# Keys and values of the fourth layer projected side by side, with a key's scaling behind the row maximum

## The chip, the cores and the metric

The kernel runs on one core of one Trainium2 chip. The metric is device time in microseconds. Five engines share the work: PE (TensorE) multiplies matrices into PSUM, DVE (VectorE) and ACT (ScalarE) read PSUM and work elementwise, POOL (GpSimd) works on SBUF alone, SP (SyncE) issues the DMAs. Each runs its own queue in order, and semaphores tie the queues together.

## What is computed

Two sequences of 256 tokens of 512 channels pass four layers, each `x + tanh(g) * attention(layernorm(x), context)` and then `x + tanh(g') * ffn(layernorm(x))`. The context has 512 rows per sequence. The change touches the attention of the fourth layer alone (32 query heads, 8 key/value heads, head size 128):

```
q = rmsnorm(hidden @ Wq.T, q_norm_w);  k = rmsnorm(context @ Wk.T, k_norm_w);  v = context @ Wv.T
rmsnorm(x, w) = x * rsqrt(mean(x*x over the 128 channels of the head) + 1e-5) * w
out = softmax(q k' / sqrt(128) + mask) v @ Wo.T
```

## The kernel before, in words

**Precision.** Every float32 matrix product is three products in fp32r: an operand is split into hi (rounded by ACT in a copy) and lo (the rest, a subtraction on DVE or POOL). The helper `three` (L365 to L372) issues hi x hi, lo x hi, hi x lo for each 128 rows of contraction. So all those matmuls have line L370.

**Tiling.** A group is one key/value head with its four query heads h = 0 to 3. The layer has 8 groups. A head has four slots j = 0 to 3, one for each 128 query rows (two per sequence). In a slot (h, j) PE does, in this order: the scores of the slot two ahead (3 matmuls of 512 columns, psS), the four transposes of this slot's probabilities (psT), at j = 0 and j = 2 the weighted sum of values for half a head (12 matmuls of 256 columns, psO), at one slot a head the projection of queries (12 of 512, psQ), and then the units of `plan(h, j)`, which use the two psX banks in turn.

**Units.** `prep` in the table ATTN names the units that make the next group's keys and values. "k" and "v" project into a tile with one channel per partition and 512 context rows across (12 matmuls of 512 columns). For the keys, ACT squares (L1131), DVE multiplies by k_norm_w into scr (L972); unit "m" sums the squares over the channels by 4 small matmuls with a tile of ones (L816), DVE and POOL turn the sums into 1/rms (L974, L1230), POOL builds diagonal tiles of it (L1234), unit "b" spreads them over the partitions by a float32 matmul (L820, two passes), DVE multiplies (L976), ACT and DVE split into hi and lo (L1138, L943). For the values, DVE copies (L982), unit "t" transposes (L811), and ACT and DVE split (L1150, L985). Units "q" (L825) are the same sums of squares for the queries; units "out" project a finished group to the output.

**What sets the order.** All of it is written out: `head` of each engine walks the same slots, and `walk` puts the groups in a hardware loop of two groups per turn (three turns) between a first and a last part; the loop goes back between slots (1,3) and (2,0). A use of a psX bank waits for the use two before it to be freed (`x_free`). The first group's units run in the prologue, one behind the other with nothing beside them. In a slot DVE does: row maximum of the slot two ahead (mask addition L897, maximum L901), the low part of the transposed probabilities (L913), the reciprocal of the row sum (L909), o_low at j = 0 (L937), then units. ACT does: high part of the transposes (L1099), exponential (L1092), o_high (L1121), units, high parts of weights. POOL does: the normalizing of a row (L1213), units, low parts of weights (1.3 us each).

Of the kernel before, what the change touches and what calls it, by code (L numbers as in the profile page):

```python
# [21 lines left out]
F32 = mybir.dt.float32  # L22
# [52 lines left out]
         prep={(1, 3): ["k0"], (2, 0): ["k1", "m0"], (2, 1): ["m1"], (2, 2): ["b0"], (2, 3): ["v0", "b1"],  # L75
               (3, 0): ["t0"], (3, 1): ["v1"], (3, 2): ["t1"]}),
# [9 lines left out]
            "av_mm o_hi o_lo x_mm x_act x_free k_f k_hi k_lo k_r k_diag").split()  # L86
# [44 lines left out]
class Layer:  # L131


    def __init__(self, index, sems):
# [24 lines left out]
        act_uses = len([u for u in self.flat if u[0] in ("t" if self.masked else "kt")])  # L159
# [6 lines left out]
                     k_f=self.n_k * n if self.masked else 0, k_hi=self.n_k * n if self.masked else 0,  # L166
                     k_lo=self.n_k * n if self.masked else 0, q_f=4 * n if self.masked else 0,
                     q_sum=4 * n if self.rope else 0, q_r=4 * n if self.rms else 0,
                     k_r=2 * n if self.rms else 0, k_diag=2 * n if self.rms else 0)
# [5 lines left out]
         self.x_free, self.k_f, self.k_hi, self.k_lo, self.k_r, self.k_diag) = counters  # L175
# [91 lines left out]
def program(nc, a, out, scratch):  # L267

    ctx = ExitStack()
    with ctx:  # L270
# [102 lines left out]


# [341 lines left out]
        def attn_tensor(pe, L):  # L716
# [160 lines left out]
        def attn_vector(dve, L):  # L877
# [67 lines left out]
            def use(g, what, gp):  # L945
# [6 lines left out]
                act_letters = "t" if L.masked else "kt"  # L952
                if kind == "t" or (kind == "k" and not L.masked):
                    L.x_act.wait(dve, L.count(g, act_letters, what))
                elif kind == "k" and L.rms:
                    L.k_f.wait(dve, L.count(g, "k", what))
# [68 lines left out]
            def head(g, h):  # L1025
                for j in range(L.slots):
                    nxt = L.step(g, h, j, L.ahead)
                    if nxt:
# [23 lines left out]
                    while late and late[0] in before:  # L1052
                        k_low(*late.pop(0))
# [25 lines left out]
        def attn_scalar(act, L):  # L1079
# [43 lines left out]
            def use(g, what, gp):  # L1123
# [3 lines left out]
                if kind in "kb":  # L1127
                    k_hi = k_cols(gp.par, i * CTX, CTX)[0]
                if kind == "k" and L.rms:
                    L.x_mm.wait(act, k + 1)  # L1130
                    L.k_f.inc(act.activation(ksq[:, i, :], X, ACT.Square))  # L1131
                elif (kind == "k" and L.rope) or kind == "b":

                    if L.rope:
                        L.k_f.wait(act, L.count(g, "k", what))
                    else:
                        L.x_free.wait(act, k + 1)
# [29 lines left out]
            def head(g, h):  # L1167
                for j in range(L.slots):
# [14 lines left out]
                    for u in L.slot_uses(g, h, j):  # L1183
                        if u[0] == "b" or (u[0] == "k" and L.rope):
# [673 lines left out]
```

How the kernel before makes its waits and increments, by code:

```python
    def wait(self, eng, value):  # L121
        if isinstance(value, int) and value <= 0:
            return
        eng.wait_ge(self.sem, value + self.base)
# [233 lines left out]
        def after(dve, ins):  # L359
            own[0] += 1
            ins.then_inc(dve_self, 1)
            dve.wait_ge(dve_self, own[0])
# [27 lines left out]
        def start_vector(dve):  # L391
            for c in range(1, DC):
                dve.wait_ge(ctx_hi, c + 1)
                dve.tensor_tensor(cT_lo[:, c, :], ctx_f[c], cT_hi[:, c, :].bitcast(F32),
                                  ALU.subtract).then_inc(ctx_lo, 1)
# [1 line left out]
        def start_scalar(act):  # L397
            act.wait_ge(gate_dma, 32)
            act.activation(gates[:, :], gates[:, :], ACT.Tanh).then_inc(gate_done, 1)
# [1 line left out]
        def start_ctx_high(act, c):  # L401
            act.wait_ge(ctx_dma[c], 16)
            act.activation(cT_hi[:, c, :], ctx_f[c], ACT.Copy).then_inc(ctx_hi, 1)
# [1 line left out]
        def start_gpsimd(pool):  # L405
            pool.wait_ge(ctx_hi, 1)
            pool.tensor_tensor(cT_lo[:, 0, :], ctx_f[0], cT_hi[:, 0, :].bitcast(F32), ALU.subtract).then_inc(ctx_lo0, 1)
# [8 lines left out]
        def dq_sync(sp, g, h):  # L416
            if g is not None and (h or g.off or g.loop is not None):
                sp.wait_ge(dq_done, g.at(4, h))
                sp.dma_start(scratch[:, bass.ds(g.address(4 * DQ, (h - 1) * DQ), DQ)], dq_w).then_inc(dq_out, 16)
            if g is None:
                sp.dma_start(dq_codes[0], a["codes"][:, 0:DQ]).then_inc(dq_code[0], 16)
# [997 lines left out]
        def f1_tensor(pe):  # L1420
            pe.wait_ge(ln_lo, 4 * NT)
```

## Time and profile before

| what | value |
|---|---|
| median of 3 runs | 2134.17 us (2130.99 to 2135.35) |
| the profiled execution | 2134.03 us, its span 2132.1 us |
| mean granted TensorE clock in the span | 0.966 |
| instructions | 33124 |

The span runs from the first to the last instruction. Busy shares are merged times of an engine. Matmuls overlap in the records, so the distance between starts tells more than a duration. A row of the timeline has the start, the duration, the engine, the line, the operation with its tiles, and in brackets the idle time ahead of it with what ended it. A row of the table by stretch has the stretch, its length, then for PE, PEld (PE's weight loads), DVE, ACT and POOL the busy time with the number of instructions, then the granted clock, the busy share of the DMA engines, and GB/s. The granted clock is 1.0 at 2.4 GHz and 0.5 at 1.2 GHz.

### The profile page before, as it was taken

The page shows a single profiled execution, that of the slowest core. Times are in us where ns is not written, and L with a number is a line of the kernel's source. Part 1 is how long each engine was busy: PE and PEld are TensorE (multiplying, and loading weights), DVE is VectorE, ACT ScalarE, POOL GpSimd, SP SyncE. Part 2 cuts the span into 40 slices and gives each one's busy share as a digit, 9 for nine tenths or more (in the row PEclk, how much of TensorE's full clock was granted, in tenths as well). Part 3 has the DMA queues.
Part 4 walks back from the last instruction along what each step waited for, and adds up shares of the span by engine and source line. Part 5 has one row for each costly group of instructions (what it writes and reads, how often), then busy time and mean ns, then how long its engine had stood idle before and what let it go on. Part 6 is the DMA issues. An engine that isn't in the chain of part 4 may idle for free.

```text
span 2132.1 us, 33124 instructions
## 1 busy us (share of the span) xinstructions
PE 1966.9 (92%) x10874; PEld 1653.4 (78%) x10874; DVE 1428.9 (67%) x2532; ACT 1035.1 (49%) x2268; POOL 951.7 (45%) x975
## 2 busy tenths in 40 slices
PE   5999999999748999998988999998799999999997
PEld 4788888888537888886766888887588888888886
DVE  5777777777768878887234555556466776677676
ACT  3766676666315545543123544542255555455442
POOL 2655555554536656663322332323154444344532
PEclk9999999999869999999988999999899999999999
DMA  3212222221301111111210101001110110111001
GB/s 141 75 46 81 84 74 78 57 74 55 99 35 54 56 54 52 61 48 51 73 48 4 34 15 28 23 1 56 55 32 30 45 46 22 40 45 45 16 20 46
DMA packets 47068, 106.76 MB, mean 50 GB/s; under 512 B 6064, under 2 KB 21936, under 8 KB 43104
## 3 DMA queue, kind: packets, MB, share of 16 engines
q1 hardware_dynamic: 46944, 105.14, 15.7%
q8 instruction: 74, 1.21, 0.2%
q14 instruction: 50, 0.41, 0.1%
HBM read 98.37 MB, written 6.75 MB: 49 GB/s over the span
## 4 chain that ended last, share of the span: by engine, by line
PE 70%; DVE 15%; issue 7%; ACT 6%; POOL 2%; DVEq 0%; ACTq 0%; POOLq 0%
PE psX L370 24%; PE psQ L370 12%; PE psS L370 12%; PE psO L370 11%; PE psT L755 6%; PE psT L370 1%; DVE pT_lo L913 1%; DVE p_sb L897 1%; DVE nbias L901 1%; ACT pT_hi L1099 1%; ACT dq_space L449 1%; ACT p_sb L1088 1%; DVE nbias L891 1%; PE psX L825 1%; ACT p_sb L1092 1%
## 5 line engine op out<-in xcount | busy, mean ns | idle before, releaser
L1213 POOL TENSOR_SCALAR p_sb<-p_sb,rrec 128x512 f32<-128x512 f32 (+1 forms) x320 | 267.0, 834 | 690.2 <-DVE rrec L909 690.2
L1099 ACT ACTIVATE pT_hi<-psT 128x512 fp32r<-128x512 f32 (+2 forms) x384 | 234.9, 612 | 349.6 <-PE psT L755 348.0
L913 DVE TENSOR_TENSOR pT_lo<-psT,pT_hi 128x512 fp32r<-128x512 f32 (+2 forms) x384 | 270.9, 705 | 107.0 <-ACT pT_hi L1099 106.4
L370 PE MATMUL psO<-pT_hi,v_hi 128*128 128x256 f32 (+1 forms) x832 | 254.6, 306 | 24.1 <-DVE pT_lo L913 18.1
L755 PE MATMUL psT<-ident,p_sb 128*128 128x128 f32 x1600 | 244.9, 278 | 14.2 <-POOL p_sb L1213 10.7
L755 PEld LDWEIGHTS psT<-ident,p_sb 128*128 128x128 f32 x1600 | 197.4, 143 | 52.8 <-POOL p_sb L1213 15.8
L370 PE MATMUL psO<-pT_lo,v_hi 128*128 128x256 f32 (+1 forms) x832 | 237.3, 285 | 0.0
L370 PE MATMUL psO<-pT_hi,v_lo 128*128 128x256 f32 (+1 forms) x832 | 237.1, 285 | 0.0
L370 PE MATMUL psQ<-xnT_hi,wq_hi 128*128 128x512 f32 (+1 forms) x448 | 189.3, 422 | 14.8 <-DVE qscr L875 9.2
L370 PE MATMUL psS<-kT_hi,q_hi 128*128 128x512 f32 (+2 forms) x448 | 177.1, 395 | 18.0 <-ACT p_sb L1092 16.1
L1092 ACT ACTIVATE p_sb<-psS,nbias 128x512 f32<-128x512 f32 (+1 forms) x192 | 145.3, 757 | 81.0 <-DVE nbias L903 81.0
L370 PE MATMUL psQ<-xnT_hi,wq_lo 128*128 128x512 f32 (+1 forms) x448 | 180.1, 402 | 0.0
L370 PE MATMUL psQ<-xnT_lo,wq_hi 128*128 128x512 f32 (+1 forms) x448 | 179.9, 402 | 0.0
L370 PEld LDWEIGHTS psO<-pT_hi,v_hi 128*128 128x128 f32 (+1 forms) x832 | 155.2, 187 | 31.1 <-DVE pT_lo L913 27.1
L370 PE MATMUL psX<-wo_hi,oT_hi 128*128 128x512 f32 (+1 forms) x432 | 172.9, 400 | 0.0
L370 PE MATMUL psX<-wo_hi,oT_lo 128*128 128x512 f32 (+1 forms) x432 | 169.5, 392 | 0.0
L370 PE MATMUL psX<-wo_lo,oT_hi 128*128 128x512 f32 (+1 forms) x432 | 169.2, 392 | 0.0
L627 POOL TENSOR_TENSOR wq_lo<-wq_f,wq_hi 128x512 fp32r<-128x512 f32 (+1 forms) x112 | 141.2, 1262 | 59.0 <-ACT wq_hi L615 59.0
L903 DVE TENSOR_REDUCE nbias<-psS 128x1 f32<-128x512 f32 (+1 forms) x192 | 147.7, 769 | 24.4 <-PE psS L370 24.2
L370 PE MATMUL psS<-kT_lo,q_hi 128*128 128x512 f32 (+2 forms) x448 | 163.7, 365 | 0.0
L370 PE MATMUL psS<-kT_hi,q_lo 128*128 128x512 f32 (+2 forms) x448 | 163.3, 364 | 0.0
L370 PE MATMUL psX<-cT_hi,wkv_hi 128*128 128x512 f32 (+1 forms) x384 | 158.0, 411 | 3.0 <-DVE kT_lo L965 1.5
(337 smaller groups left out, 4750.7 us busy)
## 6 DMA issues: line engine op xcount, KB each, us to landing
wq_f<-in_a_wq SPq DMA_DIRECT2D x96, 256.0 KB, 2.7
wo_f<-in_a_wo SPq DMA_DIRECT2D x24, 1024.0 KB, 5.7
wkv_f<-in_a_wkv SPq DMA_DIRECT2D x24, 512.0 KB, 3.8
mask_sb<-in_codes SPq DMA_DIRECT2D x32, 174.0 KB, 2.4
qscr<-in_amax SPq DMA_DIRECT2D x32, 174.0 KB, 2.3
w<-qscr SPq DMA_DIRECT2D x32, 174.0 KB, 1.8
wo_f<-in_f_wT SPq DMA_DIRECT2D x3, 1024.0 KB, 5.2
wq_f<-in_a_wq SPq DMA_DIRECT2D x16, 192.0 KB, 2.4
```

What stands on the lines that cost most here:

```text
L370: mm = pe.matmul(dst, w, m, start=(first and k == 0), stop=(last and k == n - 1))
L449: ins = act.activation(tiles[q], dq_codes[h % 2], ACT.Copy, scale=slope, bias=NF4[c] - slope * c)
L627: L.wq_lo.inc(pool.tensor_tensor(lo, f, hi.bitcast(F32), ALU.subtract))
L755: mm = pe.transpose(t_view(L, j)[:, i, :], p_view(L, j, h)[:, m * P:(m + 1) * P], ident[:, :])
L825: mm = pe.matmul(X[:, m:m + 1], qscr[:, h % 2, m * P:(m + 1) * P], ones[:, 0:1], start=True, stop=True)
L891: L.s_max.inc(dve.tensor_reduce(n, p.rearrange("p (t m) -> p t m", t=2), AX.X, ALU.max, negate=True))
L897: L.s_mask.inc(dve.scalar_tensor_tensor(p_view(L, j), s_view(L, j)[:, 0:L.open(j)], scale, mask_sb[:, t * L.keys:t * L.keys + L.open(j)], ...
L903: L.s_max.inc(dve.tensor_reduce(nbias[:, j:j + 1], s_view(L, j), AX.X, ALU.max, negate=True))
L913: L.t_lo.inc(dve.tensor_tensor(pT_view(L, pT_lo, j), t_view(L, j), pT_view(L, pT_hi, j).bitcast(F32), ALU.subtract))
L1092: L.s_exp.inc(act.activation(p_view(L, j), src, ACT.Exp, bias=nbias[:, j:j + 1], accum_out=rsum[:, j:j + 1]))
L1099: L.t_hi.inc(act.activation(pT_view(L, pT_hi, j), t_view(L, j), ACT.Copy))
L1213: L.s_norm.inc(pool.tensor_scalar(p_view(L, j), p_view(L, j), rrec[:, j:j + 1], 1.0, ALU.mult, ALU.mult))
```

## The change

In the fourth layer one unit "n" takes the place of a part of "k", "v", "m", "b" and "t". It makes 256 context rows: twice 12 matmuls of 256 columns, with 128 context rows of the context tile as weights and keys and values of the group side by side (256 columns) as the moving tile. The host lays out the weights accordingly. So one context row lies on one partition, keys in the left and values in the right half of each 256 columns. ACT squares the two key tiles with an accumulated sum (no matmul), then copies the values to v_hi; DVE subtracts for v_lo. POOL makes 1/rms from the sums (multiply and add, then power, two columns). DVE scales the keys with it into `kn` (`k_scale`), and only that frees the bank. `k_scale` stands directly behind the next slot's row maximum, except at (1,3), where it stands at the slot's end. Unit "k" then is four transposes of the scaled keys, split by ACT and DVE with k_norm_w as the multiplier. The units of the group go from k0, k1, m0, m1, b0, v0, b1, t0, v1, t1 to n0 at (1,3), n1 at (2,2), n2 at (2,3), k0 at (3,0), n3 at (3,1), k1 at (3,2). The first scores of a group wait for k0, the third for k1.

```diff
-         prep={(1, 3): ["k0"], (2, 0): ["k1", "m0"], (2, 1): ["m1"], (2, 2): ["b0"], (2, 3): ["v0", "b1"],
-               (3, 0): ["t0"], (3, 1): ["v1"], (3, 2): ["t1"]}),
+         prep={(1, 3): ["n0"], (2, 2): ["n1"], (2, 3): ["n2"], (3, 0): ["k0"], (3, 1): ["n3"], (3, 2): ["k1"]}),
...
+        ksq_tiles = ksq[:, :, :].rearrange("p a (t d) -> p (a t) d", d=P)
+        kn = scr[:, :, :].rearrange("p a (t d) -> p (a t) d", d=P)
+        wkv_rows = [z[:, :, :].rearrange("p a (c n) -> p (a c) n", n=2 * P) for z in (wkv_hi, wkv_lo)]
...
+        def halves(bank):
+            return bank.rearrange("p (t n) -> p t n", n=2 * P)
...
+                if L.rms and h == 0 and j in (0, 2):
+                    prev = g.to(-1) if g.off else None
+                    L.x_free.wait(pe, L.use(prev, f"k{b}")[0] + 1)
...
+                elif kind == "n":
+                    L.wkv_lo.wait(pe, gp.at(2, 2))
+                    for z in (0, 1):
+                        at = (2 * i + z) * P
+                        mm = three(pe, X[:, z * 2 * P:(z + 1) * 2 * P],
+                                   [([m[:, c, at:at + P] for m in (cT_hi, cT_lo)], [w[:, c, :] for w in wkv_rows])
+                                    for c in range(DC)])
+                elif kind == "k" and L.rms:
+                    L.x_free.wait(pe, L.use(g, f"n{2 * i + 1}")[0] + 1)
+                    for m in range(4):
+                        mm = pe.transpose(X[:, m * P:(m + 1) * P], kn[:, 4 * i + m, :], ident[:, :])
...
-                elif kind == "m":
-                    L.k_f.wait(pe, L.count(g, "k", f"k{i}"))
-                    for m in range(4):
-                        mm = pe.matmul(X[:, m:m + 1], ksq[:, i, m * P:(m + 1) * P], ones[:, 0:1],
-                                       start=True, stop=True)
-                elif kind == "b":
-                    L.k_diag.wait(pe, L.count(g, "b", what))
-                    mm = pe.matmul(X, ones[:, :], diag[:, :, :].rearrange("p a b -> p (a b)"), start=True, stop=True)
...
-                    ins = dve.tensor_scalar(scr[:, i, :], X, vecs[:, 1:2], None, ALU.mult)
-                elif kind == "m":
-                    ins = dve.tensor_scalar(k_ms[:, i, :], X[:, 0:4], 1.0 / hd, EPS, ALU.mult, ALU.add)
-                elif kind == "b":
-                    ins = dve.tensor_tensor(scr[:, i, :], scr[:, i, :], X, ALU.mult)
-                    late.append((g, i, kpar))
+                    ins = dve.scalar_tensor_tensor(k_lo, X, vecs[:, 1:2], k_hi.bitcast(F32), ALU.mult, ALU.subtract)
+                elif kind == "n":
+                    c = slice(2 * i * P, 2 * (i + 1) * P)
+                    dve.tensor_tensor(v_lo[:, kpar, c].rearrange("p (t d) -> p t d", d=P), halves(X)[:, :, P:2 * P],
+                                      v_hi[:, kpar, c].bitcast(F32).rearrange("p (t d) -> p t d", d=P), ALU.subtract)
+                    late.append((g, what, X))
+                    return
...
+            def k_scale(g, what, X):
+                i = int(what[1])
+                L.k_r.wait(dve, 2 * (i + 1) if g is None else g.at(8, 8 + 2 * (i + 1)))
+                L.x_free.inc(dve.tensor_tensor(kn[:, 2 * i:2 * i + 2, :], halves(X)[:, :, 0:P],
+                                               k_r[:, i // 2, 2 * (i % 2):2 * (i % 2) + 2].unsqueeze(2).broadcast_to([P, 2, P]),
+                                               ALU.mult))
...
+                    while L.rms and late:
+                        k_scale(*late.pop(0))
...
+                    while L.rms and late and (h, j) == (1, 3):
+                        k_scale(*late.pop(0))
...
-                    L.k_f.inc(act.activation(ksq[:, i, :], X, ACT.Square))
+                    for z in (0, 1):
+                        t = 2 * i + z
+                        ins = act.activation(ksq_tiles[:, t, :], halves(X)[:, z, 0:P], ACT.Square,
+                                             accum_out=k_ms[:, t // 4, t % 4:t % 4 + 1])
+                    L.k_sq.inc(ins)
+                    c = slice(2 * i * P, 2 * (i + 1) * P)
+                    L.x_act.inc(act.activation(v_hi[:, gp.par, c].rearrange("p (t d) -> p t d", d=P),
+                                               halves(X)[:, :, P:2 * P], ACT.Copy))
...
+                    elif L.rms:
+                        ins = act.activation(dst, X, ACT.Copy, scale=vecs[:, 1:2])
...
-                    L.k_r.inc(pool.tensor_tensor(k_r[:, i, :], k_ms[:, i, :], half[:, 0:4], ALU.pow))
-                    L.k_diag.inc(pool.tensor_tensor(diag[:, :, :], ident[:, :].unsqueeze(1).broadcast_to([P, 4, P]),
-                                                    k_r[:, i, :].unsqueeze(2).broadcast_to([P, 4, P]), ALU.mult))
+                    L.k_sq.wait(pool, i + 1 if g is None else g.at(4, 4 + i + 1))
+                    L.k_r.inc(pool.tensor_scalar(k_ms[at], k_ms[at], 1.0 / L.hd, EPS, ALU.mult, ALU.add))
+                    L.k_r.wait(pool, 2 * i + 1 if g is None else g.at(8, 8 + 2 * i + 1))
+                    L.k_r.inc(pool.tensor_tensor(k_r[at], k_ms[at], half[:, 0:2], ALU.pow))
...
-        arrays[f"a{i}_wkv"] = np.stack([k, v], axis=2)
+        k, v = (split(w, n).reshape(n, P, DC, hd) for w in (wk, wv))
+        arrays[f"a{i}_wkv"] = np.stack([k, v], axis=3 if i == 3 else 2).reshape(n, P, 2, DC * hd)
```

## Rows read from the trace of the kernel before

**Rows 1.** The page, its first part: busy us, share of the span, instructions.
```profile
PE 1966.9 (92%) x10874; PEld 1653.4 (78%) x10874; DVE 1428.9 (67%) x2532; ACT 1035.1 (49%) x2268; POOL 951.7 (45%) x975
```
**Rows 2.** Busy time by stretch: two groups, k0 to k0; then the prologue's units.
```profile
1642.06:1712.83 70.77, 70.67 (x415) 60.70 (x414) 50.40 (x93) 36.79 (x77) 32.41 (x34) 1.00 0.13 38
1712.83:1785.72 72.89, 71.21 (x415) 60.55 (x414) 50.50 (x93) 36.69 (x77) 32.43 (x34) 1.00 0.12 38
1515.74:1540.33 24.59, 21.56 (x97) 16.52 (x96) 7.98 (x14) 5.24 (x9) 6.37 (x6) 0.93 0.05 12
```
**Rows 3.** Timeline of PE in the fourth layer, first matmul of a unit.
```profile
1632.25 0.28 PE L370 MATMUL psO<-pT_hi,v_hi 128*128 128x256 f32 x1
...
1633.68 0.95 PE L825 MATMUL psX<-ones,qscr 128*128 128x1 f32 x8
...
1644.91 0.39 PE L370 MATMUL psS<-kT_hi,q_hi 128*128 128x512 f32 x1
...
1645.60 0.60 PE L755 MATMUL psT<-ident,p_sb 128*128 128x128 f32 x4
...
1648.27 0.47 PE L370 MATMUL psX<-cT_hi,wkv_hi 128*128 128x512 f32 x1
...
1651.12 0.95 PE L816 MATMUL psX<-ones,xn_f 128*128 128x1 f32 x8
...
1652.72 0.60 PE L755 MATMUL psT<-ident,p_sb 128*128 128x128 f32 x4
...
1657.86 0.36 PE L370 MATMUL psO<-pT_hi,v_hi 128*128 128x256 f32 x1
...
1659.37 1.02 PE L820 MATMUL psX<-rows,ones 128*128 128x512 f32 x2
...
1660.91 0.60 PE L755 MATMUL psT<-ident,p_sb 128*128 128x128 f32 x4
...
1669.50 0.60 PE L755 MATMUL psT<-ident,p_sb 128*128 128x128 f32 x4
1670.19 0.50 PE L370 MATMUL psX<-cT_hi,wkv_hi 128*128 128x512 f32 x1
```
**Rows 4.** Timeline of PE in the prologue, ahead of b0.
```profile
1525.20 1.39 PE L820 MATMUL psX<-rows,ones 128*128 128x512 f32 x2 [1.32 <-POOL rows L1234]
```
**Rows 5.** Timeline of DVE, ACT and POOL behind k0 and k1 of one group.
```profile
1646.49 0.74 DVE L897 SCALAR_TENSOR_TENSOR p_sb<-psS,q_r,mask_sb 128x512 f32<-128x512 f32 x1
...
1647.87 0.68 DVE L913 TENSOR_TENSOR pT_lo<-psT,pT_hi 128x512 fp32r<-128x512 f32 x1
...
1649.20 0.69 POOL L1213 TENSOR_SCALAR p_sb<-p_sb,rrec 128x512 f32<-128x512 f32 x1 [1.52 <-DVE rrec L909]
...
1649.93 0.15 DVE L988 TENSOR_SCALAR q_ms<-psX 128x4 f32<-128x4 f32 x1
...
1651.32 0.60 ACT L1131 ACTIVATE xn_f<-psX 128x512 f32<-128x512 f32 x1 [2.03 <-PE psX L370]
```
**Rows 6.** Timeline of DVE where the loop goes back.
```profile
1720.17 0.75 DVE L897 SCALAR_TENSOR_TENSOR p_sb<-psS,q_r,mask_sb 128x512 f32<-128x512 f32 x1 [2.83 <-issue]
```
**Rows 7.** Instructions by tile (ns min/median/max) and by line (busy us, mean ns | idle before).
```profile
L449 ACT ACTIVATE rows<-mask_sb x32: 479/482/491, 59.2 to 553.8; 128x348 f32<-128x348 int32 x32
L467 DVE TENSOR_TENSOR xn_f<-xn_f,rows x32: 509/514/517, 61.4 to 557.8; 128x348 f32<-128x348 f32 x32
...
L985 DVE TENSOR_TENSOR v_lo<-psX,v_hi 128x512 fp32r<-128x512 f32 x16 | 11.1, 692 | 6.6 <-ACT v_hi L1150 6.6
L1092 ACT ACTIVATION_READ_ACCUMULATOR p_sb<-p_sb,nbias 128x1 f32 x127 | 23.7, 186 | 0.0
L1131 ACT ACTIVATE xn_f<-psX 128x512 f32<-128x512 f32 x16 | 9.4, 588 | 13.3 <-PE psX L370 13.3
L1230 POOL TENSOR_TENSOR k_r<-k_ms,half 128x4 f32<-128x4 f32 x16 | 16.2, 1015 | 26.2 <-DVE k_ms L974 26.2
L529 POOL TENSOR_TENSOR ln_rstd<-ln_var,half 128x1 f32<-128x1 f32 x4 | 3.0, 741 | 18.0 <-DVE ln_var L489 18.0
```

More of the change, by code:

```diff
@@ L85 @@
             "q_mm q_hi q_lo q_f q_sum q_r s_mm s_mask s_max s_exp s_rec s_norm t_mm t_hi t_lo "
-            "av_mm o_hi o_lo x_mm x_act x_free k_f k_hi k_lo k_r k_diag").split()
+            "av_mm o_hi o_lo x_mm x_act x_free k_f k_hi k_lo k_sq k_r").split()
 class Group:
@@ L158, in __init__ @@
         self.total_x = len(self.first) - 4 + len(self.order) * (n - 1) + len(self.last_order) + 4
-        act_uses = len([u for u in self.flat if u[0] in ("t" if self.masked else "kt")])
+        self.act_letters = "t" if self.rope else "nk" if self.rms else "kt"
+        act_uses = len([u for u in self.flat if u[0] in self.act_letters])
         s = self.group_slots * n
@@ L165, in __init__ @@
                      x_free=self.total_x, x_act=act_uses * n, s_mask=s if self.masked else 0,
[L166 to L167 removed]
+                     k_f=self.n_k * n if self.rope else 0, k_hi=self.n_k * n if self.rope else 0,
+                     k_lo=self.n_k * n if self.rope else 0, q_f=4 * n if self.masked else 0,
                      q_sum=4 * n if self.rope else 0, q_r=4 * n if self.rms else 0,
[L169 removed]
+                     k_sq=4 * n if self.rms else 0, k_r=8 * n if self.rms else 0)
         counters = [Counter(sems[name][0], sems[name][1]) for name in COUNTERS]
@@ L174, in __init__ @@
          self.t_mm, self.t_hi, self.t_lo, self.av_mm, self.o_hi, self.o_lo, self.x_mm, self.x_act,
-         self.x_free, self.k_f, self.k_hi, self.k_lo, self.k_r, self.k_diag) = counters
+         self.x_free, self.k_f, self.k_hi, self.k_lo, self.k_sq, self.k_r) = counters
         self.wq_dma = (wqA_dma, wqB_dma)
@@ L730, in scores @@
                     if h == 0:
-                        if L.masked:
+                        if L.rope:
                             L.k_lo.wait(pe, g.at(L.n_k, L.n_k))
-                        else:
+                        elif not L.rms:
                             prev = g.to(-1) if g.off else None
                             L.x_free.wait(pe, L.use(prev, f"k{L.n_k - 1}")[0] + 1)
+                if L.rms and h == 0 and j in (0, 2):
+                    prev = g.to(-1) if g.off else None
+                    L.x_free.wait(pe, L.use(prev, f"k{b}")[0] + 1)
                 free = L.s_mask if L.masked else L.s_exp
@@ L951, in use @@
                     k_hi, k_lo = k_cols(kpar, i * CTX, CTX)
[L952 to L956, printed above, removed]
+                if kind in L.act_letters:
+                    L.x_act.wait(dve, L.count(g, L.act_letters, what))
                 else:
                     L.x_mm.wait(dve, k + 1)
-                if kind == "v" and L.masked:
+                if kind == "v" and L.rope:
                     L.k_lo.wait(dve, L.count(g, "k", f"k{i}"))
@@ L1051, in head @@
                         use(g, u, g.to(-1) if u[0] == "out" else g.to(1))
-                    while late and late[0] in before:
-                        k_low(*late.pop(0))
+                    while L.rms and late and (h, j) == (1, 3):
+                        k_scale(*late.pop(0))
             def tail(g):
@@ L1126, in use @@
                 kind, i = what[0], int(what[1])
-                if kind in "kb":
+                if kind == "k":
                     k_hi = k_cols(gp.par, i * CTX, CTX)[0]
-                if kind == "k" and L.rms:
+                if kind == "n":
                     L.x_mm.wait(act, k + 1)
-                    L.k_f.inc(act.activation(ksq[:, i, :], X, ACT.Square))
[L1132 to L1137, printed above, removed]
+                    for z in (0, 1):
[6 more added lines that the diff above has]
+                                               halves(X)[:, :, P:2 * P], ACT.Copy))
+                elif kind == "k" and L.rope:
+                    L.k_f.wait(act, L.count(g, "k", what))
                     L.k_hi.inc(act.activation(k_hi, scr[:, i, :], ACT.Copy))
@@ L1183, in head @@
                     for u in L.slot_uses(g, h, j):
-                        if u[0] == "b" or (u[0] == "k" and L.rope):
+                        if u[0] == "k" and L.rope:
                             late.append((g, u, g.to(1)))
@@ L1220, in use @@
             def use(g, what):
-                if what[0] not in "kmq" or what[0] == "out":
+                if what[0] not in "knq" or what[0] == "out":
                     return
@@ L1226, in use @@
                     L.k_f.inc(pool.tensor_tensor(scr[:, 0, :], scr[:, 0, :], scr[:, 1, :], ALU.add))
-                elif what[0] == "m":
+                elif what[0] == "n":
                     i = int(what[1])
-                    L.x_free.wait(pool, k + 1)
-                    L.k_r.inc(pool.tensor_tensor(k_r[:, i, :], k_ms[:, i, :], half[:, 0:4], ALU.pow))
-                    L.k_r.wait(pool, L.count(g, "m", what))
-                    if i:
-                        L.x_mm.wait(pool, L.use(g, "b0")[0] + 1)
-                    L.k_diag.inc(pool.tensor_tensor(diag[:, :, :], ident[:, :].unsqueeze(1).broadcast_to([P, 4, P]),
-                                                    k_r[:, i, :].unsqueeze(2).broadcast_to([P, 4, P]), ALU.mult))
+                    at = (slice(None), i // 2, slice(2 * (i % 2), 2 * (i % 2) + 2))
+                    L.k_sq.wait(pool, i + 1 if g is None else g.at(4, 4 + i + 1))
+                    pool.sem_inc(wait_met, 1)
+                    L.k_r.inc(pool.tensor_scalar(k_ms[at], k_ms[at], 1.0 / L.hd, EPS, ALU.mult, ALU.add))
+                    L.k_r.wait(pool, 2 * i + 1 if g is None else g.at(8, 8 + 2 * i + 1))
+                    L.k_r.inc(pool.tensor_tensor(k_r[at], k_ms[at], half[:, 0:2], ALU.pow))
                 elif what[0] == "q":
@@ L1784, in attn @@
         arrays[f"a{i}_wq"] = split(wq, n * G4).reshape(n * G4, P, DC * hd)
-        k, v = (split(w, n).reshape(n, P, DC * hd) for w in (wk, wv))
-        arrays[f"a{i}_wkv"] = np.stack([k, v], axis=2)
+        k, v = (split(w, n).reshape(n, P, DC, hd) for w in (wk, wv))
+        arrays[f"a{i}_wkv"] = np.stack([k, v], axis=3 if i == 3 else 2).reshape(n, P, 2, DC * hd)
         arrays[f"a{i}_wo"] = wo.reshape(n, G4, hd, D).transpose(0, 2, 1, 3)
```

3 lines of the change are left out of this document (1 added, 2 removed).

## The prediction

> **What bounds the kernel now.** First the busy shares of the page: PE is busy 92% of the span, DVE 67%, ACT 49%, POOL 45% [rows 1]. That alone says little about one layer, so next comes the table by stretch of the fourth layer [rows 2]. One steady group (four heads) takes 70.77 us, and PE is busy in 70.67 of it at granted clock 1.00. DVE has 50.4 us of work there, ACT 36.8, POOL 32.4. The reader is to see that PE has no hole. The view of waits has no entry for PE in that group; this agrees. A modelled end of a matmul can cover a small wait, so I went on to starts in the timeline [rows 3]: repeated units have constant spacing, and one pause stands out. The transposes at (3,1) start at 1669.50 and the next unit at 1670.19, 0.69 us where four transposes otherwise take 0.35: 0.34 us of waiting for the normalized row. So in this layer PE's issue sets the time. An edit is worth what it does to PE's issue, less the waits it creates.
>
> **PE, per group.** The mean durations mislead, as matmuls overlap; I use start to start [rows 3]. Removed are m0 and m1. From m1's start to the transposes behind it is 1.60 us, of which the three score matmuls are 0.69 (1644.91 to 1645.60): 0.91 each, 1.82 together (it includes the dearer restart of the matmul behind a float32 one). b0 and b1, the same way: 1660.91 - 1659.37 = 1.54, less 0.69: 0.85 each, 1.70. The transposes don't change: four of 128 columns per t unit become four per k unit.
> The projection streams the same columns in another shape: 48 matmuls of 512 columns become 96 of 256. Twelve of 512 take 2.85 us (1648.27 to 1651.12), behind a change from float32. Twelve of 256 take 1.43 (1632.25 to 1633.68), or 1.51 behind transposes (1657.86 to 1659.37). So the group goes from 4 x 2.85 = 11.40 to 8 x 1.43 + 3 x 0.08 = 11.68: +0.28. The pause of 0.34 belongs to the old b0/v0/t0 crowd on DVE in (2,3); that is lighter now, and I take the pause as gone (0 to 0.34). Net: -1.82 - 1.70 + 0.28 - 0.34 = **-3.58 us** per group.
>
> The other price of that shape is weight loads, twice as many. The rows show a 256-column matmul every 0.119 us, each with its own load, while loads average 60.70/414 = 0.147 us [rows 2, 3]: the load lies under the matmul ahead. The Trainium skill, "TensorE: Matmul & The Clock Gate", Part 3, The mechanism, says a weight load overlaps matmuls in flight "only when row_grp differs", which full-height matmuls never satisfy; by that rule the 48 extra loads would be exposed. The trace speaks against it for this form. It stays a rival below.
>
> **The other engines.** Per group DVE loses two evictions, two multiplies, two low-part subtractions from SBUF, two copies and two v_lo, and gets four subtractions and four scalings of 256 columns and two k_lo of 512. PSUM operations of 512 columns take 0.69 [rows 7]; 348 columns take 0.51, so about 1 ns a column and 0.42 for 256. That is ten passes of 512 becoming some 6.9 us: 1 us less. ACT trades four copies and two squares of 512 for eight squares of 128, four copies of 256, two of 512. All this lies beside PE and costs nothing by itself; what counts is order.
>
> **The new waits.** A scaling on DVE waits for: ACT's two squares and accumulator reads, POOL's multiply-add and power. What is queued behind it on DVE: pT_low, which the next weighted sum on PE waits for, and then the next row maximum. Durations: ACT starts 0.20 us behind the last issue of a unit (1651.12 to 1651.32) [rows 3, 5]. A square of 128 columns: 512 take 0.59, 348 take 0.48 [rows 7], hence 0.27; the read of the accumulator takes 0.19 alone, but consecutive ACT instructions overlap by 0.1, so I take 0.26 for square and read, 0.27 for the copy of 256. The power of two columns: between 0.74 (one) and 1.01 (four) [rows 7], 0.85 taken. POOL's multiply-add on two columns has no row: below it is nothing, above 1.01 (the power); nearest in kind is its tensor-scalar of 512 columns, 0.69 [rows 5], nearly all of it columns; I take 0.2. A softmax pass needs 3.40 us from its mask addition (1646.49) to the end of POOL's normalizing (1649.89) [rows 5]; slots leave it some 7.5 us.
> - n0 at (1,3), the one place where the scaling stands behind its own unit and not behind a row maximum; time 0 is n0's end of issue. The squares are done at 0.85. POOL is normalizing until 1.4, so the power ends at 2.55; the scaling runs 2.6 to 3.0. Before, row_max stood at 1646.49, 1.58 behind the end of k0 (1644.91). Now it starts at 3.0. DVE's pass of slot (2,0) takes 3.5 (1646.49 to 1649.93 and q_ms), so row_max(2,3) starts at 6.5 and pT_low(2,1) ends at 8.56. PE wants it at 8.38: slots (2,0) and (2,1) are now only 3.36 and 3.98 long. Stall 0.2.
> - n1 and n2 by the same walk: n2's scaling ends at 20.25, k0 is reached at 20.32: no stall, with no slack.
> - n3 ends at 24.8. ACT is done at 25.9, DVE's subtraction at 26.3, then row_max (1.38) and the scaling: 28.1. PE has only S, T and a weighted sum (0.69 + 0.35 + 1.51) before k1 and is there at 27.3. Stall 0.8. This is the clearest new wait: **1.0 us** per group in all, bounds 0.2 and 2.5.
> - At two groups the loop goes back just between (1,3) and (2,0). DVE there shows 2.83 us of "issue" before row_max [rows 6], and the group takes 72.89 instead of 70.77 [rows 2]. Before, that gap started at once; now it starts behind the scaling. Row_max moves to 5.8, PE waits 1.3 for the normalized row and 1.6 for pT_low: 2.9 in place of 2.12 before plus 0.2.
>
> **The prologue**, nothing beside it. Before: 1515.74 to 1540.33, 24.59 us, with a stall of 1.32 ahead of b0 [rows 2, 4], at mean clock 0.93, which is 0.14 x 24.59 = 3.4 us at 1.2 GHz, so up to 1.7 lost. After: n0, n1, n2 back to back to 1524.3, k0 to 1524.7; n3 waits for n2's scaling (2.55 behind its end) to 1526.9, ends 1529.8; k1 waits the same 2.5 to 1532.3; k1, q and the projection end at 1536.35. That is 4.0 less; the two pauses of 2.2 and 2.5 us may well bring a stretch at 1.2 GHz again, costed at 1.7: -2.3.
>
> **Sum.** Five groups at -3.58 + 1.0 = -2.6: -13.0. Two at the loop's edge: 70.77 - 3.58 + 0.8 + 2.9 = 70.9 for 72.89: -4.0. Prologue -2.3. Together -19.3, from the profiled execution's 2134.03 (span 2132.1): 2114.7. The median of the runs, 2134.17, is 0.1 above it: **2115 us**. No DMA is added or moved; SP's queue has the same loads.
>
> **Rivals.**
> 1. The waits are hidden. For it: my walk has them at 0.2, 0.0 and 0.8, small beside its errors. Then 7 x 3.6 + 4.0 = 29: 2105. Against: k1 has only 2.55 us of PE work before it.
> 2. The waits eat the gain. Each n unit holds its bank until the scaling; if stalls reach about 3 us per group, 7 x 0.6 + 2 = 6 are left: 2128. For it: DVE's queue has no slack in (3,0) to (3,2).
> 3. Slower, by the chain ACT, POOL, DVE behind each n unit at the upper bounds: squares and copy at the 512 price (+0.84), multiply-add and power at 1.01 each (+0.97), subtraction and scaling at 0.69 (+0.54). The stalls become 2.1 at pT_low, 1.5 at k0, 2.2 at k1: 5.8 against 3.58 gained, so +2.2 for seven groups and +4 in the prologue: 2153. It decides from 3.6 us of stall per group. Against: each of the three bounds is of an operation four times or more as wide, or a power.
> 4. Slower, by weight loads: were the 48 extra loads of a unit exposed at 0.147, 8 x 7.1 = 56 more: 2171. Against it are the 256-column rows. The skill's rule just cited is this rival.
>
> **Chances.** Forecast 0.60, rival 1 0.17, rival 2 0.13, rival 3 0.07, rival 4 0.03. Range: forecast's own 2108 to 2123 (stalls 0.2 to 2, pause at 1.2 GHz or not); with rivals 1 and most of 2, 2103 to 2127. A difference below 0.2% (4.3 us) can't be told from none here. Rival 2 lies about a third within it: faster 0.85, same 0.05, slower 0.10.
>
> **What would show it.** Right: group distance 68.2 us, 66 to 69; 24 matmuls of 256 in 2.86; score matmuls behind (2,1) and (2,3) back at 0.69; PE waiting for a DVE scaling ahead of the k1 transposes by 0.8, and ahead of n3 and k1 in the prologue by over 2; DVE idle before the scaling at (1,3), for POOL's power, by about a microsecond. Wrong: spacing of the 256-column matmuls above 0.14 (weight loads); PE idle over 2 us per group before k0, k1 or the weighted sum of (2,2) (the chain); POOL's multiply-add above 0.5.

## The result and the profile after

The kernel after the change takes 2119.59 us (median of 4 runs, 2118.91 to 2120.38); the one before took 2133.86 us in runs on the same chip (4 runs, 2130.99 to 2135.35). The ratio is 0.9934, interval 0.992 to 0.9947: faster by 0.66%. The forecast was 2115 us, range 2103 to 2127. The sign and the main mechanism came as forecast, and the gain was three quarters of the size: the profiled span fell from 2132.1 to 2117.6 us, by 14.5 where 19.3 was expected.

First the busy time of each engine over the whole span, which answers to [rows 1]:

```profile
PE 1945.1 (92%) x11098; PEld 1655.7 (78%) x11098; DVE 1405.4 (66%) x2516; ACT 1046.0 (49%) x2396; POOL 942.8 (45%) x1007
```

PE has 224 more matmuls and 22 us less busy time. The table by stretch of the kernel after, with the columns of [rows 2] (stretch, length, then PE, weight loads, DVE, ACT, POOL, clock): a steady group from n0 to n0, the group behind it with the loop's edge, and the prologue's units with the second projection of queries.

```profile
1638.28:1706.79 68.51, 67.91 (x443) 60.70 (x442) 47.23 (x91) 38.14 (x93) 31.41 (x38) 1.00 0.12 40
1706.79:1778.12 71.33, 68.32 (x444) 60.74 (x442) 47.31 (x91) 38.26 (x93) 31.45 (x38) 1.00 0.13 39
1514.79:1538.80 24.01, 19.68 (x125) 18.16 (x124) 5.72 (x12) 6.55 (x25) 5.86 (x10) 0.86 0.05 12
```

The steady group went from 70.77 to 68.51 us, the one at the edge from 72.89 to 71.33, the prologue from 24.59 to 24.01. PE's hole in the steady group is now 68.51 - 67.91 = 0.60 us; before it was 0.10. The view of waits for PE in that group names it:

```profile
PE psX L809 <- DVE scr L1003: 0.6, 1, 0.6
```

This is the new wait of the k1 transposes for the scaling of n3. The timeline of PE from (3,1) to (3,2) shows it, and shows a second one that the view of waits leaves out:

```profile
1662.64 0.60 PE L763 MATMUL psT<-ident,p_sb 128*128 128x128 f32 x4
1663.21 0.39 PE L372 MATMUL psX<-wkv_hi,cT_hi 128*128 128x256 f32 x1
1663.43 0.28 PE L372 MATMUL psX<-wkv_hi,cT_lo 128*128 128x256 f32 x1
...
1666.89 0.60 PE L763 MATMUL psT<-ident,p_sb 128*128 128x128 f32 x4
1667.25 0.36 PE L372 MATMUL psO<-pT_hi,v_hi 128*128 128x256 f32 x1
...
1669.51 0.66 PE L809 MATMUL psX<-ident,scr 128*128 128x128 f32 x4 [0.60 <-DVE scr L1003]
```

From its start to the next is 2.26 us for the weighted sum (1667.25 to 1669.51), where 1.51 is usual: 0.75 of waiting. And the transposes at (3,1) still take 0.57 (1662.64 to 1663.21) where the others take 0.36 (1666.89 to 1667.25): 0.21 of the old pause is left. DVE in the same stretch says why in both cases:

```profile
1663.01 0.15 DVE L997 TENSOR_SCALAR q_ms<-psX 128x4 f32<-128x4 f32 x1
...
1667.32 0.42 DVE L983 TENSOR_TENSOR v_lo<-psX,v_hi 128x256 fp32r<-128x256 f32 x1 [1.08 <-ACT v_hi L1156]
1667.66 0.74 DVE L908 SCALAR_TENSOR_TENSOR p_sb<-psS,q_r,mask_sb 128x512 f32<-128x512 f32 x1
1668.44 0.69 DVE L912 TENSOR_REDUCE nbias<-p_sb 128x1 f32<-128x512 f32 x1
1669.04 0.41 DVE L1003 TENSOR_TENSOR scr<-psX,k_r 128x256 f32<-128x256 f32 x1
```

The scaling at 1669.04 stands behind a whole row maximum and ends at 1669.45; PE starts at 1669.51. And q_ms ends at 1663.16, just ahead of n3's first matmul at 1663.21: q_ms frees the PSUM bank that n3 writes. Before, the same copy ended at 1670.14 and v1 started at 1670.19 [rows 3]:

```profile
1669.99 0.15 DVE L988 TENSOR_SCALAR q_ms<-psX 128x4 f32<-128x4 f32 x1
```

### The profile page after: what moved, and what is told of

The parts are those of the page before. It is cut to its first block, busy times and chain, and to the rows that moved or that the text cites. A ratio compares the mean times of both kernels' runs of the same rounds, so it can differ in the third digit from the quotient of the medians.

```text
span 2117.6 us, 33685 instructions
## 1 busy us (share of the span) xinstructions
PE 1945.1 (92%) x11098; PEld 1655.7 (78%) x11098; DVE 1405.4 (66%) x2516; ACT 1046.0 (49%) x2396; POOL 942.8 (45%) x1007
## 4 chain that ended last, share of the span: by engine, by line
PE 71%; DVE 13%; issue 7%; ACT 6%; POOL 2%; DVEq 0%; ACTq 0%; POOLq 0%
PE psX L372 26%; PE psQ L372 12%; PE psS L372 12%; PE psO L372 11%; PE psT L763 6%; PE psT L372 1%; DVE pT_lo L924 1%; PE psX L836 1%; ACT pT_hi L1118 1%; ACT dq_space L454 1%; ACT p_sb L1107 1%; DVE p_sb L908 1%; DVE nbias L902 1%; DVE p_sb L899 1%; POOL p_sb L1238 1%
## 5 line engine op out<-in xcount | busy, mean ns | idle before, releaser
L372 PE MATMUL psS<-kT_hi,q_hi 128*128 128x512 f32 (+2 forms) x448 | 170.5, 381 | 20.6 <-ACT p_sb L1111 16.0
L638 POOL TENSOR_TENSOR wo_lo<-wo_f,wo_hi 128x512 fp32r<-128x512 f32 (+1 forms) x112 | 148.8, 1329 | 26.9 <-ACT wo_hi L626 26.9
```

What stands on the lines that cost most here:

```text
L372: mm = pe.matmul(dst, w, m, start=(first and k == 0), stop=(last and k == n - 1))
L638: L.wo_lo.inc(pool.tensor_tensor(lo, f, hi.bitcast(F32), ALU.subtract))
```

## Experiments

Each is timed beside the kernel before, on the same chip; the ratio is to it. An L number is a line of that run's own kernel, so the copy q_ms is L988, L989 or L997.

**The shape alone.** The kernel before, with each projection as two halves of 256 columns.

```diff
-                    mm = three(pe, dst, pairs)
+                    if L.rms:
+                        for z in (0, 1):
+                            part = slice(z * 2 * P, (z + 1) * 2 * P)
+                            mm = three(pe, X[:, part], [(w, [x[:, part] for x in m]) for w, m in pairs])
+                    else:
+                        mm = three(pe, dst, pairs)
```

> The kernel before, with one part of the change alone: in the fourth layer each projection of keys or values is issued as two halves of 256 columns (24 matmuls with their own weight loads instead of 12 of 512), everything else as before. Theory (PE's issue sets the time, weight loads lie under the matmul ahead): a unit goes from 2.85 us to 24 x 0.119 + 0.08 = 2.95, so +0.4 us per group, +3 us in all: 2137, between 2134 and 2139. Rival (the doubled weight loads are exposed in part and ate some of the expected gain): at 0.147 us for each of 48 more loads per group the time goes to 2190; every 0.02 us exposed per load adds 8 us.

Measured: 2136.57 us (2135.31 to 2143.1), ratio 1.0015 (1.0006 to 1.0024). The steady group:

```profile
1648.13:1719.25 71.12, 71.12 (x463) 63.21 (x462) 50.43 (x93) 36.87 (x77) 32.37 (x34) 1.00 0.12 38
```

The profiled execution is the longest of its runs (2143.1 us), but PE is busy without a gap in this group and at clock 1.00. It is 0.35 us longer than before for 48 more weight loads; exposed, they would have added 7 us. So the new shape costs a third of a microsecond per group, and the rival of exposed loads is out. The Trainium skill, "TensorE: Matmul & The Clock Gate", Part 3, The mechanism, says that a load overlaps matmuls in flight "only when row_grp differs"; the same section also names the background weight buffer as a way for a load to be pulled ahead. For full-height loads of this form the measurement is against the first statement; the second isn't contradicted by it.

**The m and b units made short.** The kernel before, where m is one matmul of four and b streams 128 columns of 512; each row then takes the scaling factor of the first quarter, so part of the keys' scaling is left out. The passes of DVE keep their number and size (their lines aren't shown).

```diff
-                    for m in range(4):
+                    for m in range(1):
...
-                    mm = pe.matmul(X, ones[:, :], diag[:, :, :].rearrange("p a b -> p (a b)"), start=True, stop=True)
+                    mm = pe.matmul(X[:, 0:P], ones[:, :], diag[:, 0, :], start=True, stop=True)
```

> The kernel before, where unit m does one of its four matmuls and unit b spreads 128 columns instead of 512; DVE, ACT and POOL do the same number of passes of the same size (they read the one column and the 128 columns repeatedly, so the keys' scaling is that of other rows). Only PE's issue shrinks: m by 6 of 8 passes at 0.10 us (1.2 us per group), b by 0.85 to about 0.35 (1.0 per group). Theory (the gain of the change is PE's issue): -2.2 us in each of seven groups and about -1 in the prologue: 2118, between 2115 and 2123. Rival (the gain came from what DVE, ACT and POOL no longer do): no change, 2134.

Measured: 2125.6 us (2121.65 to 2128.32), ratio 0.9963 (0.9949 to 0.9976): between the theory (2115 to 2123) and the rival (2134). The group is 69.91, only 0.86 shorter. The timeline of PE at (3,1):

```profile
1664.66 0.60 PE L755 MATMUL psT<-ident,p_sb 128*128 128x128 f32 x4
...
1666.61 0.50 PE L370 MATMUL psX<-cT_hi,wkv_hi 128*128 128x512 f32 x1 [1.34 <-DVE q_ms L989]
```

and DVE there:

```profile
1666.40 0.15 DVE L989 TENSOR_SCALAR q_ms<-psX 128x4 f32<-128x4 f32 x1
```

Transposes to projection is 1.95 us now: the pause of 0.34 grew to 1.6. PE came earlier, DVE's queue did not. By starts, m, b and the scores behind b are 2.6 us shorter per group. Of that PE waits 1.25 more for q_ms, and 0.5 more one slot ahead, where the q unit needs the bank that DVE's copy of the values frees: 2.6 - 1.25 - 0.5 = 0.85. So less work on PE pays by itself, but only a third of its size. That the whole change pays more because the passes of m and b are gone from DVE too is argued from this; no run takes those passes from DVE alone. The run also shows that the pause belongs to q_ms.

**All scalings at the end of the slot.** The kernel after, with the scaling ahead of the row maximum in every slot.

```diff
-                    while L.rms and late and (h, j) == (1, 3):
+                    while L.rms and late:
```

> The changed kernel with one part undone: each key scaling stands at the end of its own slot (as the one at (1,3) does), not behind the next slot's row maximum. Theory (DVE's order makes the waits, each wait has its own slack): n3's scaling then runs at about 1.8 us behind n3's end, before k1 is reached, so the wait of 0.76 ahead of k1 goes; but DVE idles for POOL's power there and behind n2, which moves the small q_ms copy of (3,0) back by some 0.6 and lengthens the wait of 0.22 ahead of n3. Together -0.8 to +0.6 per group: 2114 to 2124, likeliest 2118. Rival (a scaling behind the row maximum is what makes the change pay, the other order puts POOL's latency on the path of the softmax): +0.9 us per scaling, three more per group, 19 us: 2139.

Measured: 2127.73 us (2126.22 to 2131.31), ratio 0.9972 (0.9962 to 0.9983); 8 us over the kernel after. In the view of waits for PE the entry at k1 is gone and another stands in its place:

```profile
PE psX L372 <- DVE q_ms L997: 1.7, 1, 1.7
```

The timeline of DVE behind n2:

```profile
1661.93 0.42 DVE L1003 TENSOR_TENSOR scr<-psX,k_r 128x256 f32<-128x256 f32 x1 [0.95 <-POOL k_r L1259]
...
1665.70 0.15 DVE L997 TENSOR_SCALAR q_ms<-psX 128x4 f32<-128x4 f32 x1
```

DVE idles 0.95 us for POOL's power before this scaling, everything behind it shifts, q_ms too, and n3's bank comes free late. By starts, the transposes at (3,1) take 2.32 us instead of 0.35 (1663.59 to 1665.91), so the pause ahead of n3 grew from 0.21 to 1.97. The wait at k1 was cured and a larger one bought: the mechanism was expected, its size was not, and the time lies above the expected 2114 to 2124.

**Only n3's scaling at the end of the slot.**

```diff
-                    while L.rms and late and (h, j) == (1, 3):
+                    while L.rms and late and (h, j) in ((1, 3), (3, 1)):
```

> The changed kernel with n3's scaling alone at the end of its slot (3,1), ahead of the next group's first row maximum; n1's and n2's stay behind theirs. Theory (two separate waits: k1 waits 0.76 for n3's scaling, n3 waits 0.2 for the bank that the q_ms copy of (3,0) frees; all scalings at the end lost 1.25 us per group because n2's pushed q_ms back by 1.8, while the wait ahead of k1 was gone): -0.76 + 0.15 for the later row maximum, -0.6 in seven groups: 2115.3 (2114 to 2117). Rival (a scaling ahead of any row maximum costs PE): 2122 or more.

Measured: 2114.28 us (2113.58 to 2114.84), ratio 0.9908 (0.9893 to 0.9923). The steady group has no hole:

```profile
1638.02:1705.89 67.87, 67.87 (x442) 60.71 (x442) 47.18 (x91) 37.77 (x93) 31.43 (x38) 1.00 0.13 40
```

It is 0.64 us shorter than after, which over seven groups is 4.5 of the 5.3 us between the medians. The timeline of DVE:

```profile
1667.70 0.42 DVE L1003 TENSOR_TENSOR scr<-psX,k_r 128x256 f32<-128x256 f32 x1 [0.48 <-POOL k_r L1259]
1668.04 0.74 DVE L908 SCALAR_TENSOR_TENSOR p_sb<-psS,q_r,mask_sb 128x512 f32<-128x512 f32 x1
```

The idle time before the scaling is 0.48 us. It ends 1.32 us behind the start of v_lo (1666.80 to 1668.12), not 2.13 as in the kernel after (1667.32 to 1669.45). The row maximum comes after it, and PE pays a little for that, though the view of waits for PE has no entry in this group. PE and DVE two slots on:

```profile
1673.24 0.60 PE L763 MATMUL psT<-ident,p_sb 128*128 128x128 f32 x4
1673.74 0.39 PE L372 MATMUL psO<-pT_hi,v_hi 128*128 128x256 f32 x1
...
1673.01 0.68 DVE L924 TENSOR_TENSOR pT_lo<-psT,pT_hi 128x512 fp32r<-128x512 f32 x1
```

The transposes at the next group's (0,0) take 0.50 us instead of 0.35, and the weighted sum starts 0.05 behind the end of pT_low (1673.69): that is the 0.15 that was expected for the later row maximum. The pause of 0.21 ahead of n3 also stays. "No hole" is what the modelled ends of the matmuls show; the starts show both.

**The last query projection one slot earlier.** q_slot (1, 1, 1, 3) becomes (1, 1, 1, 2).

> The changed kernel with the last query projection of a group one slot earlier, at (3,2), between the weighted sum and k1, so that PE has 2.83 us more to do ahead of k1. Theory: the 0.76 ahead of k1 goes, but now only four transposes and three scores lie between k1 and the third scores of the next group, which wait for k1's low part (0.2 to ACT, 0.69, DVE 0.74): a wait of 0.6 to 1.5 us shows there. Net -0.2 to +0.8 per group: 2118 to 2125. Rival (the wait ahead of k1 is all there is, the low part has room): -0.76 in seven groups, 2114.

Measured: 2131.39 us (2129.85 to 2135.44), ratio 0.9993 (0.9984 to 1.0002): nearly the whole gain is lost. The group is 69.97, and the view of waits for PE in it:

```profile
PE psS L372 <- DVE kT_lo L980: 1.2, 1, 1.2
PE psO L372 <- DVE pT_lo L924: 0.5, 1, 0.5
```

The k1 wait is gone because the 2.83 us of query projection now lie before k1. They are missing behind it, where the scores wait for the low part of the keys. By starts the two waits are 1.46 and 0.76 us; less the 0.76 at k1 that is 1.46, by which the group is longer (69.97 - 68.51). The expectation (2118 to 2125) had the first of them and missed the second. A filler moved from one wait opened another.

**n0 ahead of the loop's edge.** n0 stands in (1,2) and not in (1,3).

```diff
-         prep={(1, 3): ["n0"], (2, 2): ["n1"], ...
+         prep={(1, 2): ["n0"], (2, 2): ["n1"], ...
```

> The changed kernel with n0 one slot earlier, at (1,2), so that its scaling stands behind the row maximum of (1,3) and not between the unit and the loop's way back. Theory: the way back (some 2.7 us of issue on DVE) starts 1.4 us earlier, the two groups at the loop's edge lose 0.7 us each of the 2.8 they are longer than the others: 2118 (2116 to 2120). Rival 1 (the loop's way back costs the same wherever the scaling stands): 2119.6, unchanged. Rival 2 (slot (1,3) becomes 1.05 us short and PE waits for softmax rows in (2,0) to (2,2)): +0.3 to +1 per group, 2122 to 2127.

Measured: 2129.42 us (2127.24 to 2132.15), ratio 0.9978 (0.9969 to 0.9987). Its steady group and the one at the edge:

```profile
1639.73:1709.92 70.19, 68.09 (x443) 60.71 (x442) 47.09 (x91) 38.52 (x92) 31.51 (x39) 1.00 0.12 39
1709.92:1782.12 72.20, 68.47 (x442) 60.67 (x442) 47.16 (x91) 38.40 (x92) 31.52 (x39) 1.00 0.13 38
```

The edge's excess is 2.01 instead of 2.82 us, near the 0.7 less that the theory had. But (1,3) is a short slot without n0, and PE reaches the weighted sum of (2,0) before its operand is ready:

```profile
PE psO L372 <- DVE pT_lo L924: 1.5, 1, 1.5
```

1.7 us more in every group outweigh 0.8 less in two. That is rival 2 of the expectation, and larger than its 0.3 to 1 us per group.

**n0 ahead of the edge, with a query projection in (1,3).** q_slot is also (1, 3, 1, 3).

> The changed kernel with n0 at (1,2), as in the run that took 2129, and with head 1's query projection moved from slot (1,1) to (1,3), where n0 was. Theory (n0 at (1,2) lost 1.65 us per group because slot (1,3) was left with 1.05 us of PE work and the weighted sum of (2,0) waited for DVE's pT_low; at the loop's edge it gained 0.8): (1,3) is 4 us long again, the wait of 1.5 goes, the edge's gain stays, so -1.6 us against the changed kernel: 2118 (2116 to 2120), unless the now short slot (1,1) makes a wait of its own (up to 2123). Rival (n0 at (1,2) is bad by itself, by its bank or its scaling ahead of pT_low in (1,3)): 2127 to 2130 as before.

Measured: 2126.05 us (2124.41 to 2126.43), ratio 0.9958 (0.9944 to 0.9971), group 69.70. The wait for pT_low is 1.0 us and now stands at (1,2), behind slot (1,1), which lost its projection: the short slot moved, and the wait with it. The expectation had named that case, up to 2123; the time lies above it.

**Another order in the prologue.** n0, n1, n2, n3, k0, then the projection of queries, then k1 and the q unit.

```diff
-        self.first = self.flat + ([("q", -1)] if self.rms else [])
+        self.first = ["n0", "n1", "n2", "n3", "k0", "k1", ("q", -1)] if self.rms else self.flat
...
                 for u in L.first:
+                    if L.rms and u == "k1":
+                        q_proj(Group(0), 1)
                     use(None, u, Group(0))
-                q_proj(Group(0), 1)
+                if not L.rms:
+                    q_proj(Group(0), 1)
```

> The changed kernel with another order in the prologue alone: n0, n1, n2, n3, k0, then the second query projection (2.84 us of PE work), then k1 and q. In the changed kernel the stretch from n0 to the first scores is 24.01 us, with two pauses of about 2.2 and 2.6 us ahead of n3 and k1 and 7 us at 1.2 GHz behind them. Theory (a scaling is done 1.9 us behind its unit, so a unit or a projection between covers it; without the pauses the clock stays at 2.4 GHz): 4 x 2.88 + 0.4 + 2.84 + 0.4 + 0.8 = 16.0 us, -8: 2111.6 (2109 to 2115). Rival (the first scores aren't the bound, the softmax chain and weights behind them are, so it is given back): 2116 to 2119.6.

Measured: 2111.09 us (2109.86 to 2114.76), ratio 0.9898 (0.9882 to 0.9913). The same units and the projection:

```profile
1515.14:1531.09 15.95, 15.95 (x126) 15.40 (x125) 4.85 (x11) 6.64 (x26) 4.86 (x9) 1.00 0.06 18
```

15.95 us instead of 24.01, with neither wait and the granted clock at 1.00 up to the first scores: 8.1 of the 8.5 us between the medians.

**Both improvements.** This prologue, and n3's scaling at the slot's end.

> The changed kernel with the prologue's order n0, n1, n2, n3, k0, second query projection, k1, q, and with n3's scaling at the end of slot (3,1). Theory (the two gains are of different stretches and add): -8 and -4.3, 2107.3 (2105 to 2111). Rival (either gain is given back behind it): 2111 to 2119.

Measured: 2108.63 us (2102.75 to 2111.72), ratio 0.988 (0.9863 to 0.9897). It beats both kernels: its interval and that of the kernel after do not touch. Against the new prologue alone the intervals overlap, and only the group (67.87 us in this one too) tells them apart.

**All edits together**, that of n0 and the query projection too.

> All together: the prologue's order, n3's scaling at its slot's end, n0 at (1,2) and head 1's projection at (1,3). Theory: 2108.6 - 1.6 = 2107 (2104 to 2110). Rival (balance lost in (1,1)): 2110 to 2117.

Measured: 2113.31 us (2112.34 to 2115.3), ratio 0.9902 (0.9887 to 0.9918). The expected 2107 (2104 to 2110) was missed and the rival (2110 to 2117) was right: the moved n0 costs more than the edge gives.

## Why the prediction was right, and where it was off

**What bounds the kernel**: right. The gain is PE's issue, and in each experiment the group's length follows PE's own work and the waits of PE that the edit added or took away, read from starts.

**The sum.** Six distances from n0 to n0 give 4 x 2.26 + 2 x 1.52 = 12.1 us, the last stretch 2.3: 14.4, where the sum had 17.0 (a steady group gave 2.26, forecast 2.6; one at the edge 1.52, forecast 2.0). The prologue gave 0.58, not 2.3. Outside the sum, the layer starts 0.95 us earlier (its first projection at 1509.59 instead of 1510.54), ahead of anything that the change touches, and 1.4 were lost near the end. Of these, 1.2 are one weighted sum, which takes 2.73 us instead of 1.54. The clock of PE was low there in the kernel after and stood at 1.00 before (first the row of after, then that of before, for the same work):

```profile
2074.50:2077.90 3.40, 3.25 (x15) 3.25 (x16) 0.95 (x3) 0.82 (x3) 0.69 (x1) 0.50 0.62 215
...
2090.50:2093.90 3.40, 2.14 (x16) 1.90 (x16) 1.40 (x3) 1.33 (x4) 0.69 (x1) 1.00 0.61 212
```

14.4 + 0.58 + 0.95 - 1.4 = 14.5, the difference of the spans. Why the clock fell just there was not tested.

**The removed units**: right within the reading. They and the restarts of scores behind them took 3.5 us. The changed projection costs +0.36 (units of 2.88 to 2.98) against +0.28 forecast, and the kernel before with that shape alone showed +0.35. One more restart behind a float32 unit, q at (2,0), costs 0.08 that the sum lacked.

**The pause of 0.34 at (3,1)**: wrong. The prediction wrote "0.34 us of waiting for the normalized row" and took it as gone. It is the next unit's wait for the bank that q_ms frees. It shrank to 0.21, and it grew to 1.6 when DVE's queue was late (short m and b) and to 1.97 with all scalings at the slot's end. The row that would have told stood in the trace of before: q_ms ends 0.05 us ahead of v1. With the cause wrong, 0.2 us per group was lost from the sum, and the kernel's most sensitive place stayed unseen.

**The new waits.** Ahead of k1 0.75 measured, 0.8 forecast. At pT_low 0.08 against 0.2 (the transposes at (2,2), ahead of the weighted sum, take 0.43 for 0.35, and the sum starts at 1649.68, 0.05 behind the end of pT_low). At k0 none, as forecast. The walk held since its prices did; POOL and ACT by line and tile in the fourth layer of the kernel after:

```profile
L1259 POOL TENSOR_TENSOR k_r<-k_ms,half 128x2 f32<-128x2 f32 x32 | 22.4, 701 | 2.8 <-POOL k_ms L1257 0.2
L1257 POOL TENSOR_SCALAR k_ms<-k_ms 128x2 f32<-128x2 f32 x32 | 6.1, 192 | 11.8 <-ACT xn_f L1152 8.9
...
L1152 ACT ACTIVATE xn_f<-psX 128x128 f32<-128x128 f32 x64 | 17.1, 273 | 17.0 <-PE psX L372 17.0
```

The power of two columns takes 0.70 (0.85 taken), the multiply-add 0.19 (0.2), the square 0.27 (0.27). The upper bounds of rival 3 (1.01, 1.01, 0.59) were far off, and it fell. Rival 1 (no waits) and rival 2 (waits eat the gain) both fell; the experiments show how near rival 2 was. All scalings at their slots' ends (2127.73), n0 one slot earlier (2129.42) or one query projection one slot earlier (2131.39) each bring about its time of 2128.

Three readings of the prediction don't follow from its own terms. For DVE it wrote 1 us less per group, while ten passes at 0.69 against eight at 0.42 and two at 0.69 are 2.2 less; measured are 3.2 (50.40 to 47.23). For n0 it wrote that the power ends at 2.55, while 1.4 + 0.2 + 0.85 = 2.45; it did end at 2.45, which makes the stall at pT_low 0.1 and not 0.2. And the 48 extra loads of rival 4 are those of a group, not of a unit. The first and the last leave the sum as it is.

**The loop's edge**: the excess of that group is 71.33 - 68.51 = 2.82 us where 2.12 stood before and 70.9 - 68.2 = 2.7 was forecast. The gap of DVE now stands behind the scaling, as said:

```profile
1712.23 0.42 DVE L1003 TENSOR_TENSOR scr<-psX,k_r 128x256 f32<-128x256 f32 x1 [0.93 <-POOL k_r L1259]
1715.32 0.75 DVE L908 SCALAR_TENSOR_TENSOR p_sb<-psS,q_r,mask_sb 128x512 f32<-128x512 f32 x1 [2.67 <-issue]
```

The total came near, in part by luck. The prediction had PE wait 1.3 for the normalized row and 1.6 for pT_low. The view of waits for PE in that group:

```profile
PE psS L372 <- issue: 1.4, 1, 1.4
PE psO L372 <- DVE pT_lo L924: 1.0, 1, 1.0
```

By starts, n0 takes 4.51 us instead of 2.95 there, and the transposes at (2,2) take 1.60 instead of 0.35: 1.56 + 1.25 = 2.81. The first pause stands ahead of the scores and not of the transposes, and nothing in the profile ends it: PE too has a pause where the loop goes back. Before it was 0.22 (k0 took 3.08 for 2.85). The kernel before with the shape alone changed has it as well, with 4.39 us for k0:

```profile
PE psS L370 <- issue: 1.3, 1, 1.3
```

So this pause came with the 24 matmuls of 256 columns ahead of the loop's edge, a price of the new shape that the steady group doesn't show. It doesn't simply add to the group: with the shape alone the edge's excess is 1.89 (1719.01 to 1792.02, less 71.12). What makes it was not tested.

**The prologue**: the mis-sized term. The waits came as forecast, 1.9 ahead of n3 and 2.4 ahead of k1:

```profile
1525.94 0.38 PE L372 MATMUL psX<-wkv_hi,cT_hi 128*128 128x256 f32 x1 [1.90 <-DVE scr L1003]
...
1531.50 0.86 PE L809 MATMUL psX<-ident,scr 128*128 128x128 f32 x4 [2.43 <-DVE scr L1003]
1532.16 1.71 PE L836 MATMUL psX<-ones,qscr 128*128 128x1 f32 x8
1533.72 0.77 PE L372 MATMUL psQ<-xnT_hi,wq_hi 128*128 128x512 f32 x1
```

But the price of the low clock was put at 1.7 us, and behind the second wait it was this, from k1 to the first scores:

```profile
1531.50:1538.80 7.30, 7.30 (x24) 6.20 (x25) 0.91 (x2) 0.69 (x1) 1.01 (x1) 0.53 0.01 2
```

At a mean granted clock of 0.53, nearly all at 1.2 GHz, k1, q and projection take 7.30 us; at full clock they are 0.39 + 0.81 + 2.83 = 4.03. That is 3.3 us. The other order of the prologue, without pauses and at clock 1.00, is 8.1 us shorter; 1.9 + 2.4 + 3.3 = 7.6 of these are the two waits and the clock. By starts the two pauses are longer, 2.15 and 2.68 us (k0 takes 2.50 for 0.35, n3 takes 5.56 for 2.88), near the forecast 2.2 and 2.5, and with the clock they make up the whole 8.1.

## What to carry to other kernels

A unit taken off the bounding engine pays in full only if the engine that frees its banks keeps up: ask of each following unit which copy frees its bank, and look for a start right behind that copy's end. Put a cross-engine scaling where its operand has just arrived: a slot too early idles the queue, a row maximum too late holds up its reader, and each filler that was moved here left a short slot behind. In a prologue with nothing beside it, order the units so that the bounding engine never waits; here the pauses cost their own length and then time at the lower clock. At a loop's edge look for the pause of the bounding engine itself, not only for those of its suppliers.

## What the hardware showed unexpectedly

- A 256-column matmul with its own full-height weight load goes every 0.12 us (24 in 2.88 to 2.98); 48 extra loads cost 0.35 us in all.
- Small operations on POOL cost by kind more than by width: the power takes 0.70 us for 2 columns, 0.74 for 1 and 1.01 for 4 [rows 7], and a multiply-add on 2 columns takes 0.19.
- After pauses of 1.9 and 2.4 us in the prologue PE ran 7.3 us at a mean granted clock of 0.53; with the pauses gone it stayed at 1.00 up to the first scores.
- Where the loop goes back, DVE had 2.67 us without a start, and PE 1.4 behind a unit of 24 matmuls of 256 columns, where it had next to none behind 12 of 512 (n0 4.51 for 2.95 us, k0 before 3.08 for 2.85).
